# Loading the next batch ahead of the second attention pass, and starting a value group with its third token tile

## The chip, the cores and the metric

The kernel runs on one core of a Trainium2 chip. Its time is device microseconds (us) of one launch that works through all eight batches. A core has five instruction streams that run side by side and meet only at semaphores: TensorE (PE in the profile; PEld is its weight loads), VectorE (DVE), ScalarE (ACT), GpSimd (POOL) and SyncE (SP), which here issues nearly all transfers. The runs of the kernel before took 1346.44 us in the median of three (1345.10 to 1354.54).

## The reference, cut to what matters

Each of 8 batches is an image of 256 tokens and a text of 128 tokens, 256 features each, 384 tokens together.

```
# 1. image tokens: attention-free mixing
k, v, q = projections of x                       # x[b] is (64 features, 256 tokens, 4 heads)
num, den = exp(w_bias * mask) @ (exp(k) * v), exp(w_bias * mask) @ exp(k)
h_img = layernorm(sigmoid(q) * num / den @ out_w + out_b + x) * ln_g + ln_b
# 2. text tokens: rows of an embedding table
h_txt = W_E[tokens] * sqrt(256)
h = concat(h_img, h_txt)                         # 384 x 256
# 3. attention, 16 heads of 16, with relative keys and values in a window of +-4
s = q k^T + band(q, emb_rel_k);  p = softmax(s)
h = h + (p v + band(p) emb_rel_v) @ Wo + bo
# 4. eight experts with routing weights
h = h + sum_e w_e * (silu(x Wg_e) * (x Wu_e)) @ Wd_e
```

Batches don't depend on one another.

## The kernel before, in words

**Two batches in flight.** While a batch b goes through mixing and attention, the experts of the batch before, f = b - 1, are worked off in between, as units of matmul work with which TensorE fills the waits of the attention. The order of steps is written out by `schedule(attention, ffn)`: one list, which each engine walks, taking from it the steps for which it has a function. `rounds` (L399) puts it on an engine three times: once for batch 0 without experts, then as the body of a hardware loop `engine.Fori(1, NB)` over b = 1 to 7 with the experts of b - 1, and once more for the experts of batch 7 alone. So the loop's body runs seven times. `later(b)` tells the loop (b is a register) from batch 0 (b is a number): in the loop buffers have earlier users that must be waited for.

**One body, in order.** It begins with `residual` of batch f (output projection of its attention, L849, after the last accumulation of the experts before it, L1320), then `mix_in` of batch b: the tokens `x_in` and the text's indices `txt_idx` are transferred (L482, L483, issued by SP) and eight fp32 matmuls for exp(k), exp(k)v (L646) and four for q (L651, two records each) read x_in. Then `turn_x2` (L627 and, before it, DVE's normalisation L1075), `mix_sums`, `router`, `mix_out`, whose matmuls (L681, L684) are the last to read x_in and raise the seventh count of `mix_pe`. GpSimd gathers the text rows with the indices (L1364), scales them (L1373), and takes the roots of the normalisations (L1351, L1354). Then come the projections of q, k, v, a trip of q, k and of the relative scores through DRAM, with 20 expert units over it, the **first pass** (`maxima`, 24 items: scores for the row maxima), and the negated maxima (`negate`, in two halves, each sent to DRAM and back into two extra rows of q_st, L589 and L592).

**The second pass**, `attend`, again has 24 items. An item is two 128x384 score tiles of a head pair: TensorE multiplies (L794), VectorE adds the window of relative scores (L1187, two instructions), ScalarE takes the exponential into `p_t` (L996) and raises `exp_done`. Three pairs of PSUM banks are used in turn, so item n waits for the exponential of item n - 3. `tiles_of(n)` gives the tiles: three items hold the three token tiles (0, 1, 2) of two heads; the first holds tiles 0 and 1 of a head, the second tile 2 of both heads, the third tiles 0 and 1 of the other. No experts are worked on in this pass. Each six items (four heads) are followed by a **value group** g of three steps, `values(b, g, i)` for the token tiles i = 0, 1, 2: each is four matmuls of 17 columns of weights, for four heads, that sum over i in one bank (L809; eight records). Group g is placed behind the items 7 + 6g, 8 + 6g and 9 + 6g; its first step waits for all 6(g + 1) exponentials. Group 3 comes behind the last item, its three steps in a row. ScalarE copies each finished group (L1000). GpSimd copies the windows of p_t into `bands` (L1434), two instructions for each head pair.

**Behind the second pass** `turn_outputs` waits for the last copy. SP sends the windows to DRAM and back in another layout (L600, L609), and `turn_weights` (DVE L1207, then TensorE) takes them. Between these steps lie the last expert units of batch f. The body ends with `store` on SP (L616), which waits for the last accumulation. SP works in order, so in the next turn of the loop the transfer of x_in is issued behind that store:

```
def mix_in(b):                                   # SP, L477
    if later(b):
        sp.wait_ge(mix_pe.sem, mix_pe.at(b - 1, 7))
        sp.wait_ge(txt_loaded.sem, txt_loaded.at(b - 1, 1))
    sp.dma_start(x_in[0:F, :, :], a["x"][b]).then_inc(x_loaded.sem, 16)
    sp.dma_start(txt_idx[:], a["txt_t"][b]).then_inc(idx_loaded.sem, 16)
```

Of the kernel before, what the change touches and what calls it, by code (L numbers as in the profile page):

```python
# [33 lines left out]
NB = 8  # L34
F, L, H = 64, 256, 4
# [4 lines left out]
TT = T // P  # L40
IT = L // P
AH, AD = 16, 16
# [24 lines left out]
GRP = 4  # L67
PTS = 6
# [12 lines left out]
FILL_MAXIMA = [0, 0, 0, 1, 0, 0, 0, 1, 0, 0, 0, 1, 0, 0, 0, 1, 0, 0, 0, 1, 0, 0, 0, 0]  # L81
FILL_NEGATE = 2
# [18 lines left out]
def fusion_block(nc, a, out):  # L101
# [14 lines left out]
    with ctx:  # L116
# [203 lines left out]
        def schedule(attention, ffn):  # L320
# [50 lines left out]
            flush()  # L371
            for n in range(ITEMS):
                steps.append(("attend", n, dict(seen)))


                g, at = divmod(n - 7, 6)
                if g >= 0 and at < TT:
                    steps.append(("values", g, at, dict(seen)))
                if n >= 9 and (n - 9) % 6 == 0:
                    steps.append(("copy", (n - 9) // 6))  # L380
            last = AH // GRP - 1
            steps += [("values", last, i, dict(seen)) for i in range(TT)] + [("copy", last)]
# [16 lines left out]
        def rounds(engine, parts):  # L399
# [9 lines left out]
            with engine.Fori(1, NB) as b:  # L409
                for s in schedule(True, True):  # L410
                    do(s, b, b - 1)
            for s in schedule(False, True):
                do(s, None, NB - 1)
# [8 lines left out]
        def later(b):  # L422

            return not isinstance(b, int)
# [5 lines left out]
        def _(sp):  # L430
# [45 lines left out]

            def mix_in(b):  # L477

                if later(b):
                    sp.wait_ge(mix_pe.sem, mix_pe.at(b - 1, 7))  # L480
                    sp.wait_ge(txt_loaded.sem, txt_loaded.at(b - 1, 1))
                sp.dma_start(x_in[0:F, :, :], a["x"][b]).then_inc(x_loaded.sem, 16)  # L482
                sp.dma_start(txt_idx[:], a["txt_t"][b]).then_inc(idx_loaded.sem, 16)  # L483
                if not later(b):
                    load(1)
# [132 lines left out]
            rounds(sp, {"mix_in": mix_in, "prepare": prepare, "project_rel": project_rel,  # L618
# [6 lines left out]
        def _(pe):  # L625
# [172 lines left out]
            def values(b, g, i, seen):  # L798

                if i == 0:  # L800
                    pe.wait_ge(exp_done.sem, exp_done.at(b, 6 * (g + 1)))
# [5 lines left out]
                for l in range(GRP):  # L807
                    h = GRP * g + l
                    mm = pe.matmul(S[32 * l:32 * l + VC, 6 + g % 2, 0:T], v_one[:, i, h, :],  # L809
                                   p_t[:, h % PTS, i, :], start=(i == 0), stop=(i == TT - 1),  # L810
                                   skip_group_check=True)
                if i == TT - 1:
                    mm.then_inc(pv_done.sem, 1)
# [228 lines left out]
        def _(dve):  # L1042
# [267 lines left out]
            def accumulate(f, e, part):  # L1310
# [4 lines left out]
                if last and part == 0 and not isinstance(f, int):  # L1315
# [167 lines left out]
```

## Time and profile before

| | |
|---|---|
| time, median of 3 runs | 1346.44 us (1345.10 to 1354.54) |
| the profiled execution | 1361.19 us, its span 1359.4 us |
| TensorE busy, of the span | 1139.8 us, 84% |
| VectorE, ScalarE, GpSimd busy | 750.2, 370.3, 234.3 us |
| granted TensorE clock, mean | 0.896 of full speed |
| stores of the batches 0 to 6 issued at | 327.43, 484.87, 645.17, 802.26, 964.96, 1123.16, 1279.74 us |

The profile is of one execution, which was 14.75 us above the median of the timed runs. A timeline row gives start, duration, engine, line and operation, and in brackets how long the engine had been idle before it and what ended that. A granted clock of 1.00 is TensorE at 2.4 GHz, 0.50 at 1.2 GHz. The distance between two stores is one turn of the loop: 156.6 to 162.7 us.

### The profile page before, as it was taken

The page shows a single profiled execution, that of the slowest core. Times are in us where ns is not written, and L with a number is a line of the kernel's source. Part 1 is how long each engine was busy: PE and PEld are TensorE (multiplying, and loading weights), DVE is VectorE, ACT ScalarE, POOL GpSimd, SP SyncE. Part 2 cuts the span into 40 slices and gives each one's busy share as a digit, 9 for nine tenths or more (in the row PEclk, how much of TensorE's full clock was granted, in tenths as well). Part 3 has the DMA queues.
Part 4 walks back from the last instruction along what each step waited for, and adds up shares of the span by engine and source line. Part 5 has one row for each costly group of instructions (what it writes and reads, how often), then busy time and mean ns, then how long its engine had stood idle before and what let it go on. Part 6 is the DMA issues. An engine that isn't in the chain of part 4 may idle for free.

```text
span 1359.4 us, 16898 instructions
## 1 busy us (share of the span) xinstructions
PE 1139.8 (84%) x5668; PEld 801.1 (59%) x5668; DVE 750.2 (55%) x1579; ACT 370.3 (27%) x599; POOL 234.3 (17%) x258
## 2 busy tenths in 40 slices
PE   5447689878898798988899788997999889898798
PEld 4311379526784377735785277852787457762587
DVE  6336363673547546484546735485454745567443
ACT  1204312062211622134120621216121351205211
POOL 5404220031200402012200412004020122003100
PEclk9667779898999988899898987998889997999989
DMA  6592207402092102901065020921119010460200
GB/s 221 145 202 77 44 5 111 107 1 60 1 168 49 36 24 54 162 1 36 24 103 114 1 59 0 164 54 29 30 48 168 2 36 24 84 133 1 47 0 12
DMA packets 126842, 89.59 MB, mean 66 GB/s; under 512 B 67847, under 2 KB 116360, under 8 KB 126378
## 3 DMA queue, kind: packets, MB, share of 16 engines
q1 hardware_dynamic: 126408, 88.05, 31.9%
q0 software_dynamic: 384, 1.05, 0.3%
q14 instruction: 39, 0.32, 0.1%
q8 instruction: 11, 0.18, 0.1%
HBM read 60.36 MB, written 28.71 MB: 66 GB/s over the span
## 4 chain that ended last, share of the span: by engine, by line
PE 32%; issue 26%; DVE 15%; DMA 12%; SPq 6%; ACT 5%; POOL 3%; POOLq 0%; DVEq 0%; ACTq 0%
DMA scratch<-d_band_t 9%; PE S L878 7%; PE S L754 5%; PE S L746 4%; DVE S L1187 4%; PE S L899 4%; SPq L538 4%; PE S L809 4%; ACT scratch L996 3%; PE S L710 3%; DVE maxima L1166 3%; PE S L794 2%; DMA txt_row<-in_L_txt_W_E,txt_idx 1%; PE S L627 1%; DMA w_d<-in_L_ffn_Wu 1%
## 5 line engine op out<-in xcount | busy, mean ns | idle before, releaser
L1166 DVE TENSOR_REDUCE maxima<-S 128x2 f32<-128x768 f32 x192 | 177.1, 954 | 86.7 <-PE S L754 83.9
L1434 POOL TENSOR_TENSOR bands<-scratch,one 64x432 f32<-64x432 f32 x128 | 119.7, 935 | 598.3 <-ACT scratch L996 593.2
L899 PE MATMUL S<-w_d,hT 128*128 128x256 f32 x768 | 189.4, 395 | 1.6 <-DVE hT L1308 0.7
L746 PE MATMUL S<-k_st,q_st 128*128 128x384 bf16 x384 | 140.7, 366 | 49.3 <-DMA scratch<-d_band_t 35.6
L1033 ACT ACTIVATE silu<-S 128x384 f32<-128x384 f32 x128 | 63.0, 492 | 436.2 <-PE S L878 382.1
L1187 DVE TENSOR_TENSOR S<-S,bands 64x144 f32<-64x144 f32 x384 | 154.5, 402 | 44.7 <-PE S L794 35.0
L996 ACT ACTIVATE scratch<-S 128x768 f32<-128x768 f32 x192 | 155.7, 812 | 56.6 <-DVE S L1187 49.2
L899 PEld LDWEIGHTS S<-w_d,hT 128*128 128x128 f32 x768 | 150.5, 199 | 25.0 <-issue 3.7
L754 PE MATMUL S<-scratch,ident_b 128*128 128x132 bf16 (+1 forms) x384 | 155.0, 404 | 0.0
L1308 DVE TENSOR_TENSOR hT<-silu,S 128x384 f32<-128x384 f32 x128 | 70.7, 552 | 130.5 <-PE S L878 120.7
L794 PE MATMUL S<-q_st,k_st 128*128 128x384 bf16 x384 | 94.0, 344 | 35.7 <-ACT scratch L996 34.5
L809 PE MATMUL S<-scratch,v_one 128*17 128x384 f32 x768 | 91.9, 574 | 27.4 <-ACT scratch L996 27.1
L746 PEld LDWEIGHTS S<-k_st,q_st 128*128 128x128 bf16 x384 | 39.5, 103 | 120.2 <-DVE maxima L1166 59.0
L1320 DVE SCALAR_TENSOR_TENSOR res<-S,wgt,res 128x256 f32<-128x256 f32 x168 | 75.4, 480 | 48.3 <-PE S L899 48.0
L794 PEld LDWEIGHTS S<-q_st,k_st 128*128 128x128 bf16 x384 | 25.6, 98 | 122.5 <-ACT scratch L996 92.5
L878 PE MATMUL S<-x_hi,wu_hi 128*128 128x384 f32 x256 | 77.1, 384 | 15.0 <-DVE hT L1308 15.0
L878 PE MATMUL S<-x_hi,wg_hi 128*128 128x384 f32 x256 | 81.7, 402 | 0.0
L627 PE MATMUL S<-ident,scratch 128*128 128x128 f32 (+1 forms) x196 | 36.7, 338 | 42.9 <-DVE scratch L1075 28.6
L878 PE MATMUL S<-x_lo,wg_hi 128*128 128x384 f32 x256 | 68.9, 352 | 0.0
L878 PE MATMUL S<-x_hi,wg_lo 128*128 128x384 f32 x256 | 68.5, 350 | 0.0
L878 PE MATMUL S<-x_lo,wu_hi 128*128 128x384 f32 x256 | 68.1, 348 | 0.0
L878 PE MATMUL S<-x_hi,wu_lo 128*128 128x384 f32 x256 | 67.9, 347 | 0.0
(157 smaller groups left out, 1488.4 us busy)
## 6 DMA issues: line engine op xcount, KB each, us to landing
bands<-d_band_s SPq DMA_DIRECT2D x16, 864.0 KB, 8.7
scratch<-d_band_t SPq DMA_DIRECT2D x8, 1632.0 KB, 16.9
d_parts<-scratch SPq DMA_DIRECT2D x48, 192.0 KB, 2.0
q_st<-d_parts SPq DMA_DIRECT2D x48, 192.0 KB
k_st<-d_parts SPq DMA_DIRECT2D x48, 192.0 KB
d_band_w<-bands SPq DMA_DIRECT2D x32, 240.0 KB, 3.8
out<-scratch SPq DMA_DIRECT2D x8, 384.0 KB, 2.5
x_in<-in_x SPq DMA_DIRECT2D x8, 256.0 KB, 3.6
```

The source lines that it names most:

```text
L746: pe.matmul(S[:, bank, PAD:PAD + T], q_st[:, h, i * P:(i + 1) * P], k_st[:, h, :], start=True, stop=False, skip_group_check=True)
L754: mm = pe.matmul(S[rows, bank, at + w0:at + w1], ident_b[rows, rows], band_t[rows, i, w0:w1, h], start=False, stop=True, skip_group_check= ...
L794: mm = pe.matmul(S[:, 2 * (n % 3) + l, PAD:PAD + T], k_st[:, h, i * P:(i + 1) * P], q_st[:, h, :], start=True, stop=True)
L809: mm = pe.matmul(S[32 * l:32 * l + VC, 6 + g % 2, 0:T], v_one[:, i, h, :], p_t[:, h % PTS, i, :], start=(i == 0), stop=(i == TT - 1), skip ...
L878: mm = pe.matmul(dst[:, 0:T], ws[:, e, k, m * P:(m + 1) * P], xs[:, k, :], start=(j == 0), stop=(j == 3 * KT - 1))
L899: mm = pe.matmul(D[:, i // 2, (i % 2) * E:(i % 2 + 1) * E], hT[:, (FT * e + m) % 3, i * P:(i + 1) * P], w_d[:, e, m, :], start=(m == 0), s ...
L996: nc.scalar.activation(dst, S[:, c0:c0 + 2, PAD:PAD + T], ACT.Exp).then_inc(exp_done.sem, 1)
L1166: dve.tensor_reduce(dst, S[:, c0:c0 + 2, PAD:PAD + T], AX, ALU.max).then_inc(max_done.sem, 1)
L1187: dve.tensor_tensor(win, win, band, ALU.add).then_inc(sc_add.sem, 1)
L1308: dve.tensor_tensor(hT[:, n % 3], silu[:], U[:, 0:T], ALU.mult).then_inc(h_done.sem, 1)
L1320: dve.scalar_tensor_tensor((out_st if last else res)[:, i], D[:, i // 2, (i % 2) * E:(i % 2 + 1) * E], wgt[:, i, e:e + 1], res[:, i], ALU. ...
L1434: nc.gpsimd.tensor_tensor(bands[rows, :, :, 2 * pair:2 * pair + 2].rearrange("p i w h -> p h i w"), win, one[rows].unsqueeze(2).unsqueeze( ...
```

## The change

The step list gets a new step `fetch` between the negated maxima and the second pass: SP then transfers the tokens and indices of batch b + 1, after waiting for `mix_out` and the text gather of batch b. `mix_in` keeps the transfer for batch 0 only. Batch 7 has nothing to fetch, so the loop runs to b = 6, and the turn b = 7 is written out behind it with `more=False`. Within a value group the order of token tiles is 2, 0, 1. The first step (tile 2) waits for one exponential fewer, the second for all of the group; the accumulation starts with tile 2 and ends with tile 1. In group 3 tile 2 comes right behind the last item. `later` now also holds for a number above zero, and a wait in VectorE's last accumulation holds for f = 6 as it did in the loop.

```diff
+VALUE_TILES = (2, 0, 1)
...
-        def schedule(attention, ffn):
+        def schedule(attention, ffn, more=True):
...
             fill(FILL_NEGATE)
             flush()
+            if more:
+                steps.append(("fetch",))
             for n in range(ITEMS):
                 steps.append(("attend", n, dict(seen)))
+                if n == ITEMS - 1:
+                    steps.append(("values", AH // GRP - 1, VALUE_TILES[0], dict(seen)))
                 g, at = divmod(n - 7, 6)
                 if g >= 0 and at < TT:
-                    steps.append(("values", g, at, dict(seen)))
+                    steps.append(("values", g, VALUE_TILES[at], dict(seen)))
                 if n >= 9 and (n - 9) % 6 == 0:
                     steps.append(("copy", (n - 9) // 6))
             last = AH // GRP - 1
-            steps += [("values", last, i, dict(seen)) for i in range(TT)] + [("copy", last)]
+            steps += [("values", last, i, dict(seen)) for i in VALUE_TILES[1:]] + [("copy", last)]
...
-            with engine.Fori(1, NB) as b:
+            with engine.Fori(1, NB - 1) as b:
                 for s in schedule(True, True):
                     do(s, b, b - 1)
+            for s in schedule(True, True, False):
+                do(s, NB - 1, NB - 2)
...
-            return not isinstance(b, int)
+            return not isinstance(b, int) or b > 0
...
-            def mix_in(b):
-
-                if later(b):
-                    sp.wait_ge(mix_pe.sem, mix_pe.at(b - 1, 7))
-                    sp.wait_ge(txt_loaded.sem, txt_loaded.at(b - 1, 1))
+            def load_x(b):
                 sp.dma_start(x_in[0:F, :, :], a["x"][b]).then_inc(x_loaded.sem, 16)
                 sp.dma_start(txt_idx[:], a["txt_t"][b]).then_inc(idx_loaded.sem, 16)
+
+            def fetch(b):
+
+                sp.wait_ge(mix_pe.sem, mix_pe.at(b, 7))
+                sp.wait_ge(txt_loaded.sem, txt_loaded.at(b, 1))
+                load_x(b + 1)
+
+            def mix_in(b):
+
                 if not later(b):
+                    load_x(b)
                     load(1)
                     load(2)
...
             def values(b, g, i, seen):
-                if i == 0:
-                    pe.wait_ge(exp_done.sem, exp_done.at(b, 6 * (g + 1)))
+                if i != VALUE_TILES[-1]:
+
+                    pe.wait_ge(exp_done.sem, exp_done.at(b, 6 * (g + 1) - (i == VALUE_TILES[0])))
+                if i == VALUE_TILES[0]:
                     if g >= 2:
                         pe.wait_ge(o_copied.sem, o_copied.at(b, g - 1))
...
-                                   p_t[:, h % PTS, i, :], start=(i == 0), stop=(i == TT - 1),
+                                   p_t[:, h % PTS, i, :], start=(i == VALUE_TILES[0]), stop=(i == VALUE_TILES[-1]),
                                    skip_group_check=True)
-                if i == TT - 1:
+                if i == VALUE_TILES[-1]:
                     mm.then_inc(pv_done.sem, 1)
...
-                if last and part == 0 and not isinstance(f, int):
+                if last and part == 0 and not (isinstance(f, int) and f == NB - 1):
```

## Rows read from the trace of the kernel before

**Rows 1.** The page: busy time of the engines; ScalarE's exponentials.
```profile
PE 1139.8 (84%) x5668; PEld 801.1 (59%) x5668; DVE 750.2 (55%) x1579; ACT 370.3 (27%) x599; POOL 234.3 (17%) x258
...
L996 ACT ACTIVATE scratch<-S 128x768 f32<-128x768 f32 x192 | 155.7, 812 | 56.6 <-DVE S L1187 49.2
```

**Rows 2.** TensorE's waits, 169 to 1286, seven turns: total, times, longest.
```profile
PE S L794 <- ACT scratch L996: 32.0, 62, 1.2
PE S L809 <- ACT scratch L996: 24.1, 26, 2.4
...
PE S L646 <- DMA x_in<-in_x: 11.8, 6, 2.0
```

**Rows 3.** Timeline at a turn's start: start, us, engine, line [idle before].
```profile
327.31 2.86 PE L849 MATMUL S<-w_o,scratch 128*128 128x256 f32 x12 [1.03 <-DVE scratch L1320]
...
328.50 0.55 SPq L482 DMA_DIRECT2D x_in<-in_x  x1
...
332.07 4.10 PE L646 MATMUL S<-wkv,x_in 65*128 65x128 f32 x16 [1.91 <-DMA x_in<-in_x]
...
332.51 0.86 POOL L1354 TENSOR_TENSOR rstd<-rstd,neg_half 128x3 f32<-128x3 f32 x1
...
336.10 2.06 PE L651 MATMUL S<-x_in,wq_t 65*64 65x256 f32 x8
...
336.96 1.15 DVE L1075 TENSOR_SCALAR scratch<-res,mv,rstd 128x256 f32<-128x256 f32 x3
...
338.17 1.54 PE L627 MATMUL S<-ident,scratch 128*128 128x128 f32 x6
```

**Rows 4.** Timeline, the last transfer of `negate` before the second pass, batch 2.
```profile
436.25 0.23 SPq L592 DMA_DIRECT2D q_st<-d_neg  x1
```

**Rows 5.** The tile x_in: from issue to landing.
```profile
DMA to landing us min/median/max: 3.4/3.6/3.7
```

**Rows 6.** Timeline of a second pass: first items, value groups 0 to 2.
```profile
437.34 1.24 PE L794 MATMUL S<-q_st,k_st 128*128 128x384 bf16 x6
...
444.17 0.84 PE L809 MATMUL S<-scratch,v_one 128*17 128x384 f32 x8 [0.46 <-ACT scratch L996]
...
444.94 0.50 PE L794 MATMUL S<-q_st,k_st 128*128 128x384 bf16 x2
...
450.48 0.84 PE L809 MATMUL S<-scratch,v_one 128*17 128x384 f32 x8 [0.32 <-ACT scratch L996]
...
456.87 0.84 PE L809 MATMUL S<-scratch,v_one 128*17 128x384 f32 x8 [0.41 <-ACT scratch L996]
```

**Rows 7.** Timeline, end of second passes: last exponentials, value group 3.
```profile
461.48 1.65 ACT L996 ACTIVATE scratch<-S 128x768 f32<-128x768 f32 x2
...
463.26 3.82 PE L809 MATMUL S<-scratch,v_one 128*17 128x384 f32 x24 [2.39 <-ACT scratch L996]
...
1259.82 2.13 PE L809 MATMUL S<-scratch,v_one 128*17 128x384 f32 x24 [2.38 <-ACT scratch L996]
```

**Rows 8.** Timeline, the windows' way back: batch 2 in the loop, batch 0.
```profile
471.05 1.80 SPq L609 DMA_DIRECT2D scratch<-d_band_w  x3
...
477.12 0.67 DVE L1207 TENSOR_TENSOR scratch<-scratch 128x216 f32<-128x216 f32 x2
...
153.86 1.76 SPq L609 DMA_DIRECT2D scratch<-d_band_w  x3
...
158.01 0.68 DVE L1207 TENSOR_TENSOR scratch<-scratch 128x216 f32<-128x216 f32 x2 [4.82 <-DMA scratch<-d_band_w]
```

**Rows 9.** Stretches, two turns and group 3: us, busy by engine, clock, DMA, GB/s.
```profile
649.82:806.98 157.16, 136.33 (x709) 96.00 (x709) 91.52 (x196) 45.20 (x74) 24.92 (x30) 0.95 0.32 60
806.98:969.62 162.64, 143.43 (x709) 100.42 (x709) 91.43 (x195) 45.41 (x74) 24.87 (x30) 0.88 0.31 58
...
463.20:467.70 4.50, 3.83 (x25) 0.95 (x25) 0.00 (x0) 0.54 (x2) 1.86 (x2) 0.62 0.36 75
```

**Rows 10.** DMA queue that brings instructions, 325 to 490: packets, MB, share.
```profile
q14 instruction: 7, 0.06, 0.1%
```

More of the change, by code:

```diff
@@ L616, in store @@
                 sp.dma_start(out[f].rearrange("(i p) e -> p i e", p=P), out_st).then_inc(stored.sem, 16)
-            rounds(sp, {"mix_in": mix_in, "prepare": prepare, "project_rel": project_rel,
+            rounds(sp, {"mix_in": mix_in, "fetch": fetch, "prepare": prepare, "project_rel": project_rel,
                         "weights": weights, "negate": negate, "turn_weights": windows_back,
```

## The prediction

> **What bounds the kernel now.** I read the page first. TensorE is busy for 84% of the span and no other engine reaches 60% [rows 1]. So the kernel is near TensorE's own work, and what an edit can win is a hole in TensorE that nothing refills. The list of waits tells which holes exist. In the seven turns of the loop the largest are waits for ScalarE's exponentials, ahead of the items of the second pass (32.0 us) and ahead of the value groups (24.1 us), then for x_in (11.8 us) [rows 2]. The change touches the second and the third. The timelines then say where each hole lies and what stands behind it.
>
> **Part 1, the tokens of the next batch.** At a turn's start TensorE ends the output projection about 330.2 (327.31 + 2.86) and then stands until 332.07, because SP issued x_in only at 328.50, behind the store [rows 3]; the landing takes 3.6 us [rows 5], and 328.50 + 3.6 is 332.1. The waits are six in number, 1.9 to 2.0 us each, 11.8 us in sum [rows 2]. The seventh turn start, b = 1, has no such wait, because batch 0 has no experts and no store, so nothing is counted there. After the change x_in has landed long before, and the matmuls L646 begin at 330.2.
>
> Is the shift kept? Behind L646 come L651 (336.10) and the transposes L627 (338.17), which follow L651 without a hole (336.10 + 2.06 = 338.16) [rows 3]. The transposes need DVE's normalisation L1075, which stood at 336.96 behind the products of exp(k); those follow L646 and move with it. It also needs GpSimd's roots, done at 333.37 (332.51 + 0.86), where the moved L1075 wants them at 335.0, so there are 1.6 us to spare [rows 3]. GpSimd's gather of the text stands behind those roots in an unchanged order and needs no x_in; the first reader of its rows is the statistics of the whole batch, behind mix_out. I take the full 11.8 us. The ends are 0, if a second late operand stands right behind, and 11.8 plus nothing: more than the wait can't come out of the wait.
>
> What the moved step costs where it goes: per batch two waits and two transfers on SP behind the last transfer of `negate`, at 436.5 [rows 4]. Both waits are for steps that lie before the projections and the first pass, so nothing queued behind them is held; SP's next own step is the windows' way out, behind the last exponential at 463.1 [rows 7]. 256 KB in flight for 3.6 us share the queues with the small transfer of the negated maxima, issued just ahead and needed in its second half only from item 12, over 10 us on. Cost 0; were that cover gone it would be at most the 3.6 us of one landing.
>
> **Part 2, the first wait of value groups 0 to 2.** The first step of a group stood 0.46, 0.32 and 0.41 us for an exponential [rows 6], in sum 1.19 us a pass. With tile 2 first the exponential it needs is one that the item ahead of it has already waited for, so the wait is gone; the step takes 0.77 us (444.17 to the next item at 444.94) [rows 6], and in that time the missing exponential ends, which the next item and the second step need. So the next item starts 0.4 us earlier and, since TensorE is then the engine the others wait for (0.77 us of values ahead of each of three items), the whole chain behind it moves. I followed the recurrence item by item (TensorE 0.43 us for an item, DVE 0.85, ScalarE 0.83, a step 0.77, three bank pairs, the copy and the gate of p_t slots included): it gives 25.8 us from the first item to the last exponential where the trace has 25.8 (437.34 [rows 6] to 463.13 [rows 7]), and 24.6 with the new order. So 1.2 us a pass is kept. ScalarE's own work doesn't stop it: 24 exponentials of 0.81 us are 19.5 us [rows 1].
>
> **Part 3, value group 3.** Before, TensorE stood 2.39 us until the last exponential, then ran three steps in 3.82 us [rows 7]. The exponentials of the last two items are back to back (461.48, 1.65 us for two), so the last but one ends about 0.8 us before the last [rows 7], and a step of 0.77 us fits into that. Two steps remain behind the last exponential instead of three: the gain is a third of the group's time. Over the eight passes that time is 3.72, 3.68, 3.82 (four times), 3.17 and 2.13 us. It is 3.82 where the granted clock is at its low level, 1.2 GHz, for most of it (mean 0.62 from 463.2 on [rows 9]) and 2.13 at 2.4 GHz. In the seven loop passes the sum is 24.3 us, a third of it 8.1.
>
> Is it kept behind the pass? The last copy, `turn_outputs` and expert units follow on TensorE. What runs in parallel is the windows' way: GpSimd's last windows, SP's two trips. It starts with the last exponential, so it moves by 1.2 us, while TensorE moves by 1.2 plus 0.7 to 1.3. In batch 0 the second trip is issued at 153.86 and DVE gets it at 158.01, 4.15 us on [rows 8]; in the loop 471.05 + 4.15 is 475.2, and DVE takes it at 477.12 [rows 8], so 1.9 us are to spare and at least 0.6 stay. Kept in the loop. In batch 0, without expert units, that way is itself the path (DVE waits 4.82 us for it [rows 8]), so only the 1.2 us of part 2 count there.
>
> **Part 4, the last turn written out.** The same instructions with numbers in place of registers, and one jump back fewer. At the jump TensorE waited 1.03 us, and for DVE's last accumulation, not for instructions [rows 3]; I count 0, with 0 to 1.03 as bounds on the good side. On the bad side there is new code to bring in: seven packets of instructions in a turn, of 8 KB each [rows 10]. They come in loop turns as well, under running work. The Trainium skill ("Runtime: NRT & Kernel Launch", Instruction fetch mechanics) says that a taken branch breaks the sequential prefetch and forces a fetch before execution goes on; by it the missing jump would add a little to the gain. No row here shows such a stall, so the sum goes without it.
>
> **The sum.** 11.8 (x_in) + 7 x 1.19 = 8.3 (groups 0 to 2) + 8.1 (group 3) + 1.2 (batch 0) = 29.4 us. The profiled execution of 1361.19 us would come to 1331.8. It stood 14.75 us, 1.1%, above the median; against the median of 1346.44 the same 29.4 us give **1317 us**. All parts act on waits that exist in every execution, only group 3 depends on the clock.
>
> **The clock is the unknown size.** Two turns with the same 709 matmuls took 157.16 and 162.64 us, at mean granted clocks of 0.95 and 0.88 [rows 9]. The three timed runs lie 9 us apart. A change that moves work by 2 to 4 us a turn changes where the low stretches fall. If every loop turn fell like the shortest, the six turns from 327.43 to 1279.74, 158.7 on average, would each give 1.6 us more, 11 us over seven; if like the longest, they would lose 3.9 each, 27 us. The Trainium skill ("TensorE: Matmul & The Clock Gate", Part 1) says that for modelling the ramp's penalty is under 1% of a typical span. By that both ends would stay within 13 us. The trace differs: 5.5 us between two turns is 3.4% of a turn. I keep the wider bounds for the rivals and half of them for the likeliest case.
>
> **Rivals.**
> 1. *The second pass gives its share back.* Items wait for ScalarE 32.0 us already [rows 2]; if removed group waits reappear ahead of items, parts 2 and 3 bring nothing and only x_in remains: 1346.4 - 11.8 = 1335. For it: the pass is a ring of three engines, and each group's wait is for the engine that also gates the items. Against it: the items behind a group's steps start without a wait [rows 6], so there TensorE leads. Chance 0.10.
> 2. *More than the waits.* Fewer holes, so the clock stays up: 1317 - 11 = 1306. For it: at a second pass's end, behind a hole of 2.39 us, the mean was 0.62 [rows 7, 9]. Against: the low stretches at turn starts also came after holes that stay (1.03 us [rows 3]). Chance 0.10.
> 3. *The clock takes it back.* All turns fall like the longest: 1317 + 27 = 1344. Against: turns differ among each other and will again. Chance 0.06.
> 4. *Slower: fetching the written-out turn.* Its code runs once, straight through, on five engines. If each of its 8 KB packets held TensorE for a landing like x_in's, 3.6 us [rows 5], the seven of a turn would cost 25 us [rows 10], and twice as many packets (straight code is not kept) 50 us: 1317 + 50 = 1367. It decides from nine held packets on (29.4 + 1% of 1346 is 43 us, twelve packets, for slower by over 1%). Against: batch 0 is straight code too, and its second pass has the same group waits and period as the loop's. Chance 0.04.
>
> **How the numbers follow.** The forecast, both parts kept, has 0.70; its own range is 1309 to 1331, half the clock bounds around 1317. The range to give takes in rivals 1 and 2: 1303 to 1336; about 0.12 lies outside, mostly rivals 3 and 4. A measurement of this kernel tells about 1% from no change, so faster means under 1333: the forecast and rival 2 and a small part of rival 1, 0.82. Within 1%: the rest of rival 1, rival 3 and a tail, 0.14. Slower: 0.04.
>
> **What the profile after would show.** TensorE's wait for x_in is gone, and L646 follows L849 at once; SP's L482 of the next batch stands right behind L592. The first step of value groups 0 to 2 starts without a wait, a second pass takes 24.6 us from first item to last exponential, and group 3 appears as one step ahead of the last exponential and two behind it. Wrong would be: a wait of some 2 us for another releaser ahead of L646 or ahead of L627 at 1075's place; waits ahead of L794 grown by what L809's fell; DVE's L1207 waiting for the windows in the loop; a hole of TensorE without a releaser in the last turn.

## The result and the profile after

The changed kernel takes 1300.18 us (median of 4 runs, 1298.56 to 1307.80), the kernel before 1350.49 us beside it: a ratio of 0.966, with a 95% interval of 0.960 to 0.971. Timed again in five rounds it took 1299.09 us, ratio 0.964 (0.959 to 0.969). The ratio leaves out runs over 1.5% above the kernel's fastest, here the 1361.05 us of the kernel before, and gives 46 to 48 us; the medians alone give 50. The forecast said 29. So its 1317 us had the direction and missed the size, and its range, 1303 to 1336, ended 3 us above the measured median.

The page after: VectorE, ScalarE and GpSimd are busy within 2 us as long as before. TensorE is busy 31 us less (1139.8 to 1109.1) with the same 5668 matmuls, so they ran faster. Of the 62 us between the two profiled executions the other 31 are TensorE's holes (span less busy time, 219.6 to 188.2). Two lines of the page, the first answering to [rows 1]:

```profile
PE 1109.1 (85%) x5668; PEld 787.9 (61%) x5668; DVE 748.5 (58%) x1579; ACT 369.6 (28%) x599; POOL 233.8 (18%) x258
...
L824 PE MATMUL S<-scratch,v_one 128*17 128x384 f32 x768 | 81.3, 507 | 12.3 <-ACT scratch L1011 12.3
```

TensorE's waits after, in seven turns (160 to 1230), answering to [rows 2], and behind them two of the kernel before (169 to 1286) that [rows 2] leaves out. Total, times, longest:

```profile
PE S L807 <- ACT scratch L1011: 32.3, 63, 1.2
PE S L640 <- DVE scratch L1090: 18.5, 8, 4.3
PE S L824 <- ACT scratch L1011: 10.8, 7, 1.6
...
PE S L759 <- DMA scratch<-d_band_t: 4.6, 5, 1.3
...
PE S L627 <- DVE scratch L1075: 14.3, 7, 2.1
...
PE S L746 <- DMA scratch<-d_band_t: 11.0, 7, 3.4
```

The wait for x_in is gone, that ahead of the value groups fell from 24.1 to 10.8 us and occurs seven times instead of 26, and the items' own waits (now L807) did not grow: 32.0 before, 32.3 after. That settles rival 1: nothing was given back inside the second pass. The wait ahead of the transposes (L627, now L640) did not change either: 14.3 us in seven turns, and 4.3 us once behind them, at 1225.63, for the last batch's experts, where no mixing lies between.

The wait for the relative scores (`d_band_t`, the transfer ahead of the first pass) fell from 11.0 to 4.6 us, and neither part of the change touches it. It is 2.4 us in the profile of experiment 1, which has every wait of the kernel before, so it differs by 8.6 us between executions of the same work. The difference of 6.4 us is not to be counted for the change.

The turn's start after, answering to [rows 3]; the matmuls on x_in are now L659 and L664, the transposes L640:

```profile
467.60 2.86 PE L864 MATMUL S<-w_o,scratch 128*128 128x256 f32 x12 [1.03 <-DVE scratch L1335]
470.29 3.85 PE L659 MATMUL S<-wkv,x_in 65*128 65x128 f32 x16
474.07 2.06 PE L664 MATMUL S<-x_in,wq_t 65*64 65x256 f32 x8
476.06 1.54 PE L640 MATMUL S<-ident,scratch 128*128 128x128 f32 x6
```

L659 follows L864 without a hole, and from the output projection to the transposes it is 8.46 us, against 10.86 before. The transfer stands where it was put, behind the negated maxima [rows 4]:

```profile
423.02 0.23 SPq L605 DMA_DIRECT2D q_st<-d_neg  x1
423.59 0.55 SPq L485 DMA_DIRECT2D x_in<-in_x  x1
```

The same second pass as in [rows 6] and [rows 7], after. It begins at 424.02, and the first steps of groups 0, 1 and 2 carry no wait:

```profile
424.02 1.24 PE L807 MATMUL S<-q_st,k_st 128*128 128x384 bf16 x6
...
430.32 0.84 PE L824 MATMUL S<-scratch,v_one 128*17 128x384 f32 x8
431.10 0.50 PE L807 MATMUL S<-q_st,k_st 128*128 128x384 bf16 x2
...
436.23 0.84 PE L824 MATMUL S<-scratch,v_one 128*17 128x384 f32 x8
...
442.15 0.84 PE L824 MATMUL S<-scratch,v_one 128*17 128x384 f32 x8
...
447.71 2.22 PE L824 MATMUL S<-scratch,v_one 128*17 128x384 f32 x24 [1.56 <-ACT scratch L1011]
```

Groups 0 to 2 now follow each other in 5.9 us (430.32, 436.23, 442.15) where they took 6.3 and 6.4. Group 3 starts behind a hole of 1.56 us and takes 2.22 us instead of 3.82. Where each turn of the loop spends less can be read from the first rows of each stage. The table has the seven turns in sum, from the timelines of four profiled executions: before (1361.19 us), experiment 1 (the same waits as before, 1337.44 us), after (1299.13 us) and experiment 12 (the changed kernel again, 1298.74 us).

| stretch of a turn | before | exp. 1 | after | exp. 12 |
|---|---|---|---|---|
| output projection to mix_sums | 85.5 | 85.4 | 69.8 | 69.8 |
| mix_sums to the projections of q, k | 215.8 | 214.4 | 210.8 | 213.0 |
| projections to the first pass | 246.6 | 238.4 | 239.8 | 240.2 |
| first pass | 198.2 | 188.4 | 189.7 | 189.8 |
| to the second pass | 37.3 | 33.7 | 36.8 | 35.5 |
| second pass with group 3 | 208.8 | 210.3 | 185.7 | 182.6 |
| behind it | 123.9 | 124.2 | 124.0 | 123.8 |

The first row is the fetch, the sixth the order of tiles. The rows between them were touched by neither part. They lose 21 us from before to after, but the profiled execution of before was one of its slower ones; against experiment 1, the fastest of its runs, they lose nothing that two executions of one kernel do not differ by. So most of the gain lies in the two rows that the change touches: 15.7 us in the first and 23 to 28 in the sixth, 39 to 43 together, where the forecast had 11.8 and 16.4, or 28. The medians of all runs differ by 50 us, so some 7 to 11 us of a typical execution lie in other stretches; these four profiles don't show where.

Turns of the loop after, with the clock, against [rows 9]; and group 3:

```profile
467.60:617.60 150.00, 134.82 (x708) 96.90 (x708) 91.20 (x195) 45.14 (x74) 24.80 (x30) 0.97 0.33 63
768.80:919.10 150.30, 135.61 (x709) 96.12 (x709) 91.18 (x195) 45.05 (x74) 24.82 (x30) 0.97 0.33 63
447.70:450.50 2.80, 2.22 (x24) 0.50 (x24) 0.00 (x0) 1.18 (x2) 1.86 (x2) 1.00 0.00 0
```

The mean granted clock of the whole execution is 0.93, against 0.896. In group 3 it is 1.00, against 0.62 in [rows 9].

### The profile page after: what moved, and what is told of

Read it like the earlier page. It is cut to its first block, busy times and chain, and to the rows that moved or that the text cites. A ratio compares the mean times of both kernels' runs of the same rounds, so it can differ in the third digit from the quotient of the medians.

```text
span 1297.3 us, 16627 instructions
## 1 busy us (share of the span) xinstructions
PE 1109.1 (85%) x5668; PEld 787.9 (61%) x5668; DVE 748.5 (58%) x1579; ACT 369.6 (28%) x599; POOL 233.8 (18%) x258
## 4 chain that ended last, share of the span: by engine, by line
PE 40%; issue 22%; DVE 16%; DMA 10%; SPq 5%; ACT 4%; POOL 3%; POOLq 0%; DVEq 0%; ACTq 0%
PE S L893 10%; DMA scratch<-d_band_t 6%; PE S L914 6%; PE S L767 5%; PE S L759 4%; DVE S L1202 4%; PE S L824 4%; PE S L723 3%; DVE maxima L1181 3%; PE S L807 3%; SPq L551 3%; ACT scratch L1011 3%; PE S L640 2%; DMA txt_row<-in_L_txt_W_E,txt_idx 1%; DMA w_d<-in_L_ffn_Wu 1%
## 5 line engine op out<-in xcount | busy, mean ns | idle before, releaser
L914 PE MATMUL S<-w_d,hT 128*128 128x256 f32 x768 | 184.4, 388 | 1.4 <-DVE hT L1323 0.7
L759 PE MATMUL S<-k_st,q_st 128*128 128x384 bf16 x384 | 134.4, 350 | 45.0 <-DMA scratch<-d_band_t 29.8
L1011 ACT ACTIVATE scratch<-S 128x768 f32<-128x768 f32 x192 | 155.5, 811 | 44.9 <-DVE S L1202 37.3
L914 PEld LDWEIGHTS S<-w_d,hT 128*128 128x128 f32 x768 | 147.8, 195 | 23.8 <-issue 2.3
L807 PE MATMUL S<-q_st,k_st 128*128 128x384 bf16 x384 | 93.1, 341 | 36.1 <-ACT scratch L1011 34.8
L807 PEld LDWEIGHTS S<-q_st,k_st 128*128 128x128 bf16 x384 | 25.6, 98 | 122.1 <-ACT scratch L1011 96.3
L824 PE MATMUL S<-scratch,v_one 128*17 128x384 f32 x768 | 81.3, 507 | 12.3 <-ACT scratch L1011 12.3
L893 PE MATMUL S<-x_hi,wu_hi 128*128 128x384 f32 x256 | 76.8, 382 | 12.9 <-DVE hT L1323 12.8
L893 PE MATMUL S<-x_hi,wg_hi 128*128 128x384 f32 x256 | 80.8, 397 | 0.0
L640 PE MATMUL S<-ident,scratch 128*128 128x128 f32 (+1 forms) x196 | 34.2, 321 | 45.2 <-DVE scratch L1090 28.6
L893 PE MATMUL S<-x_lo,wu_hi 128*128 128x384 f32 x256 | 68.6, 350 | 0.0
L893 PE MATMUL S<-x_hi,wu_lo 128*128 128x384 f32 x256 | 68.4, 350 | 0.0
L893 PE MATMUL S<-x_lo,wg_hi 128*128 128x384 f32 x256 | 67.7, 346 | 0.0
L893 PE MATMUL S<-x_hi,wg_lo 128*128 128x384 f32 x256 | 66.4, 341 | 0.0
```

Of the source, the lines that this page charges most:

```text
L759: pe.matmul(S[:, bank, PAD:PAD + T], q_st[:, h, i * P:(i + 1) * P], k_st[:, h, :], start=True, stop=False, skip_group_check=True)
L807: mm = pe.matmul(S[:, 2 * (n % 3) + l, PAD:PAD + T], k_st[:, h, i * P:(i + 1) * P], q_st[:, h, :], start=True, stop=True)
L893: mm = pe.matmul(dst[:, 0:T], ws[:, e, k, m * P:(m + 1) * P], xs[:, k, :], start=(j == 0), stop=(j == 3 * KT - 1))
L914: mm = pe.matmul(D[:, i // 2, (i % 2) * E:(i % 2 + 1) * E], hT[:, (FT * e + m) % 3, i * P:(i + 1) * P], w_d[:, e, m, :], start=(m == 0), s ...
L1011: nc.scalar.activation(dst, S[:, c0:c0 + 2, PAD:PAD + T], ACT.Exp).then_inc(exp_done.sem, 1)
```

## The experiments

The theory under test, "waits and clock": each closed hole gives its own length, and the rest comes from TensorE spending less time at 1.2 GHz. Rivals: "waits only", and for the missing 17 us the code written out.

**1. The last turn written out and nothing else.** The kernel before, with:

```diff
-            with engine.Fori(1, NB) as b:
+            with engine.Fori(1, NB - 1) as b:
                 for s in schedule(True, True):
                     do(s, b, b - 1)
+            for s in schedule(True, True):
+                do(s, NB - 1, NB - 2)
...
-            return not isinstance(b, int)
+            return not isinstance(b, int) or b > 0
...
-                if last and part == 0 and not isinstance(f, int):
+                if last and part == 0 and not (isinstance(f, int) and f == NB - 1):
```

> The kernel before with its seventh loop turn written out and nothing else. The whole change gained about 46 us (ratio 0.966) where the removed waits explain 29. Theory 'waits and clock' (each hole closed gives its own length, and the rest comes from TensorE staying at its high clock): this kernel has every hole of before, so 1350 us, ratio 0.995 to 1.005. Rival 'written-out code' (the missing 17 us come from the straight turn): ratio about 0.987. Rival 'straight code must be fetched': ratio over 1.005.

Measured: 1349.24 us, ratio 1.0004 (0.997 to 1.004). Neither a gain nor a cost of fetching the written-out turn beyond the interval, 5 us each way; rival 4 (25 to 50 us) and the rival for the missing part (17 us) both fall. Its runs also showed how far one and the same program spreads, 1337 to 1363 us.

**2. The fetch alone.** Tokens ahead, value groups in the old order; against the changed kernel:

```diff
-VALUE_TILES = (2, 0, 1)
+VALUE_TILES = (0, 1, 2)
...
-                if n == ITEMS - 1:
-                    steps.append(("values", AH // GRP - 1, VALUE_TILES[0], dict(seen)))
...
-            steps += [("values", last, i, dict(seen)) for i in VALUE_TILES[1:]] + [("copy", last)]
+            steps += [("values", last, i, dict(seen)) for i in VALUE_TILES] + [("copy", last)]
...
-                if i != VALUE_TILES[-1]:
-
-                    pe.wait_ge(exp_done.sem, exp_done.at(b, 6 * (g + 1) - (i == VALUE_TILES[0])))
+                if i == VALUE_TILES[0]:
+                    pe.wait_ge(exp_done.sem, exp_done.at(b, 6 * (g + 1)))
```

> Tokens fetched ahead and the last turn written out; value groups in the old order 0, 1, 2. Theory 'waits only': the six waits of L646, 11.8 us, so ratio 0.991. Theory 'waits and clock': more than the waits, 15 to 22 us, ratio 0.984 to 0.989, with TensorE's low-clock time clearly under the 284 us of the profile before.

Measured: 1324.29 us, ratio 0.979 (0.974 to 0.984): 28 to 29 us for waits of 11.8 us, more than the 15 to 22 that "waits and clock" had expected. Value group 3, behind its old hole of 2.4 us, is as slow as before in five of the seven turns (3.58 to 3.82 us) and takes 2.13 us in two. The first of the slow ones:

```profile
297.13 3.58 PE L821 MATMUL S<-scratch,v_one 128*17 128x384 f32 x24 [2.37 <-ACT scratch L1008]
```

**3. The order alone.** The kernel before with `values` and the step list of the change, x_in as before, all turns in the loop.

> Only the order of the value tiles (2, 0, 1); tokens loaded as before, all seven turns in the loop. Theory 'waits only': 8.3 + 8.1 + 1.2 = 17.6 us, ratio 0.987. Theory 'waits and clock': 23 to 32 us, ratio 0.976 to 0.983, with value group 3 in 2.2 us instead of 3.8 in most turns.

Measured: 1318.69 us, ratio 0.9755 (0.971 to 0.980), 33 us for 17.6 of waits and a step. Here second passes, counted from the first item to the end of group 3, take 25.9 to 26.0 us in five of seven turns; with the whole change it is four of seven in the first profile and six of seven in experiment 12. By the ratios the two parts won 29 and 33 us alone and 46 to 48 together. Waits that lie in different stages would be expected to add up; that these don't fits a clock that both parts raise, but does not show it.

**4. Group 3 late again, in the changed kernel.**

```diff
-                    pe.wait_ge(exp_done.sem, exp_done.at(b, 6 * (g + 1) - (i == VALUE_TILES[0])))
+                    pe.wait_ge(exp_done.sem, exp_done.at(b, 6 * (g + 1) - (i == VALUE_TILES[0] and g < 3)))
```

> The changed kernel, but the first step of value group 3 again waits for the last exponential, so three steps follow it in a row behind a hole of 2.4 us; groups 0 to 2 and the fetch stay. Theory 'waits only': it loses the 8 us of one step a turn against the changed kernel, ratio to before 0.972. Theory 'waits and clock': the hole of 2.4 us lowers the clock again, group 3 takes 3.8 us, and it loses 14 us or more, ratio 0.976 or above.

Measured: 1303.81 us, ratio 0.966 (0.960 to 0.972). Both theories missed: against the changed kernel it costs 4 to 5 us by the medians and 0 to 2 by the ratios, which is not clear of the noise and less than either said. Its timeline at group 3, in four of the seven turns:

```profile
295.43 2.13 PE L824 MATMUL S<-scratch,v_one 128*17 128x384 f32 x24 [2.38 <-ACT scratch L1011]
444.78 2.13 PE L824 MATMUL S<-scratch,v_one 128*17 128x384 f32 x24 [2.39 <-ACT scratch L1011]
595.68 2.13 PE L824 MATMUL S<-scratch,v_one 128*17 128x384 f32 x24 [2.38 <-ACT scratch L1011]
...
896.92 3.44 PE L824 MATMUL S<-scratch,v_one 128*17 128x384 f32 x24 [2.39 <-ACT scratch L1011]
```

The hole is as long as before, and yet the group runs at the high clock (1.00 from 444.70 to 447.50), in six of the seven turns. So the hole of 2.4 us by itself does not bring the low clock; something ahead of it has to be as it was. Experiment 2 narrows it down: it too has the fetch and this hole, but groups 0 to 2 wait as before, and there group 3 is slow in five of seven turns. What differs is groups 0 to 2, which in experiment 2 start behind waits of 0.3 to 0.5 us and here without (and the order of the tiles in them).

**5. Holes filled, waits kept.** The kernel before; TensorE multiplies into a bank that the next matmul overwrites, ahead of L646 and ahead of group 3. No wait is shortened.

```diff
+            def busy(bank, n):
+                for _ in range(n):
+                    pe.matmul(S[:, bank, 0:E], w_o[:, 0, 0:P], w_o[:, 0, :], start=True, stop=True,
+                              skip_group_check=True)
...
+                if later(b):
+                    busy(0, 3)
                 pe.wait_ge(x_loaded.sem, x_loaded.at(b, 1))
...
+                if i == 0 and g == 3:
+                    busy(7, 4)
+                    pe.wait_ge(exp_done.sem, exp_done.at(b, 6 * (g + 1)))
```

> The kernel before, with both waits left in place but filled: three idle-result fp32 matmuls (128x128 by 128x256, some 1.4 us) in TensorE's hole ahead of L646 in the loop turns, and four (some 1.9 us) in the hole of 2.4 us ahead of value group 3. Their results are overwritten. No wait of the change is shortened. Theory 'waits and clock': the clock stays up more, and at least a third of the 46 us comes back without any edit of the waits: ratio 0.975 to 0.99. Theory 'waits only': 0 or a little slower, ratio 0.998 to 1.005.

Measured: 1335.87 us, ratio 0.988 (0.984 to 0.992). This shows the clock's part without any change of the waits: work that nobody needs, put into two of them, makes the kernel 16 us faster.

**6. Groups 0 to 2 late again, in the changed kernel.** `i == VALUE_TILES[0] and g == 3` in the place of experiment 4's condition.

> The changed kernel, but the first step of value groups 0 to 2 waits for all of its group's exponentials as before; fetch and the early step of group 3 stay. Part 2 of the sum was 8.3 us: 'waits only' expects 0.6 points more than the changed kernel, ratio 0.972. 'Waits and clock' expects the second pass to be 1.2 us longer a turn and the low clock to come back at group 3 in part of the turns: ratio 0.972 to 0.978.

Measured: 1312.29 us, ratio 0.970 (0.967 to 0.974), 12 to 13 us slower than the changed kernel by the medians, 6 to 8 by the ratios, where the sum had 8.3. TensorE's waits ahead of L824 are 18.5 us again, 27 times. Second passes take 27.3 us in six of seven turns, 1.4 longer than with the change. The low clock did not come back at group 3, as "waits and clock" had expected: group 3 takes 2.2 to 2.3 us in every turn, and the mean clock of the runs, 0.931, is above the changed kernel's 0.926. TensorE also waits 13.8 us ahead of expert units (L893), against 10.3, but that wait is 10.9 to 14.2 us in profiles of kernels with every wait of before.

**7. Holes filled in the changed kernel.** `busy` ahead of the output projection (2), of the transposes of the normalised tokens (3) and of group 3's early step (2).

> The changed kernel with idle-result fp32 matmuls in three holes that are left: two ahead of the output projection, three ahead of the transposes of the normalised tokens, two ahead of the early step of group 3. 'Waits and clock': low-clock time falls below the 184 us of the changed kernel's profile and the time by up to 10 us, unless the added matmuls delay the path: ratio 0.96 to 0.968. 'Waits only': 0 to 5 us slower, ratio 0.966 to 0.970.

Measured: 1304.51 us, ratio 0.964 (0.960 to 0.968). The ratio lies inside the range of "waits and clock", but its interval holds the changed kernel's own, so this tells nothing apart. The mean clock did not rise either (0.928 in the profiled execution, against 0.930 and 0.926 in the two of the changed kernel), so filling these holes gave nothing that can be measured.

**8. One expert unit earlier, in the changed kernel.** `("router_pick", 2)` in the place of 1.

> The changed kernel with one more expert unit behind router_pick, in TensorE's hole of 2.1 us ahead of the transposes, and so one fewer at the turn's end. Every theory: 1.0 us a turn is won if the hole takes it, about 7 us, ratio 0.960; if VectorE's accumulation, which then comes ahead of its normalisation, delays that, nothing or a loss: 0.966 to 0.970.

Measured: 1330.97 us, ratio 0.985 (0.981 to 0.988): 31 us slower than the changed kernel. TensorE's waits in seven turns show why; two of these rows the changed kernel does not have, VectorE's accumulation ahead of the transposes and the negated maxima ahead of an expert's down part:

```profile
PE S L893 <- DVE hT L1323: 16.3, 13, 1.7
PE S L640 <- DVE res L1335: 11.5, 6, 1.9
PE S L640 <- DVE scratch L1090: 9.6, 7, 1.4
...
PE S L914 <- DVE neg_max L1186: 8.5, 7, 1.2
```

A unit moved at one place shifts every later one, and other kinds of unit then stand at the tight places: between the passes a turn needs 8.0 us instead of 5.3, and the seven first passes 204.8 us instead of 189.7. Of the 32 us between the profiled executions 27 are TensorE's holes (215.1 against 188.2), and 5 are matmuls that ran slower.

**9 and 10. Each hole filled alone, in the kernel before.** Experiment 5 without `busy(0, 3)`, and without `busy(7, 4)`.

> The kernel before with only the hole ahead of value group 3 filled (four fp32 matmuls whose result is overwritten), all waits as before. With both holes filled the ratio was 0.988. If the clock lost at group 3 is what the filling wins, each turn's second pass is 1.7 us shorter (28.0 against 29.7 us) and the ratio 0.990 to 0.993; if the hole at the turn's start is the one that counts, 0.996 to 1.001.

> The kernel before with only the hole ahead of L646 filled (three fp32 matmuls whose result is overwritten), x_in still waited for. If the idle TensorE at the turn's start is what pulls the clock down in the mixing stage, ratio 0.990 to 0.995 and low-clock time from a turn's start to the projections of 10 us a turn instead of the 14 to 20 in every other turn of before; if not, 0.998 to 1.003.

Measured: group 3 alone 1334.60 us, ratio 0.9895 (0.982 to 0.997); the turn's start alone 1355.50 us, ratio 1.002 (0.999 to 1.006). The gain of filling lies at group 3; at the turn's start it is 2 us at most, by the interval. Its timeline there, with the four matmuls (L640, eight records) in the hole:

```profile
451.44 0.82 PE L799 MATMUL S<-q_st,k_st 128*128 128x384 bf16 x4
452.11 1.89 PE L640 MATMUL S<-w_o 128*128 128x256 f32 x8
454.60 2.13 PE L818 MATMUL S<-scratch,v_one 128*17 128x384 f32 x24 [0.60 <-ACT scratch L1005]
```

The group is released as late as before and takes 2.13 us instead of 3.82. Its stretch shows the granted clock at 1.00:

```profile
454.50:457.30 2.80, 2.13 (x24) 0.60 (x24) 0.00 (x0) 0.54 (x2) 1.88 (x2) 1.00 0.00 0
```

It won 14 us by the ratio (4 to 24 by its interval), where seven groups of 1.7 us less make 12. At the turn's start the filling was there too, leaving 0.6 to 1.0 us of the wait:

```profile
479.33 1.46 PE L640 MATMUL S<-w_o 128*128 128x256 f32 x6
481.38 2.83 PE L653 MATMUL S<-wkv,x_in 65*128 65x128 f32 x11 [0.59 <-DMA x_in<-in_x]
```

Here the clock did rise, from a mean of 0.74 to 0.79 in the old turn starts to 0.87 to 0.91 in six of the seven, between the output projection and mix_sums, and it bought nothing: these turns need 12.1 to 12.5 us to mix_sums as before. x_in still lands when it did, L646's matmuls ran at the high clock for the most part already (4.10 us against 4.00), and the transposes behind them wait up to 0.15 us for VectorE. In the turn b = 1, which has no such wait, the three matmuls are plain extra work and cost 1.3 us.

**11. Mixing ahead of the output projection.** The early tokens allow it: in the step list `mix_in` comes first, with the waits that the shared banks and GpSimd's windows then need.

```diff
-FILL_MIX = [("residual", 0), ("mix_in", 0), ("turn_x2", 0), ...
+FILL_MIX = [("mix_in", 0), ("residual", 0), ("turn_x2", 0), ...
...
+                if later(b):
+                    pe.wait_ge(att_dve.sem, att_dve.at(b - 1, 2 * TT + 2 * KT))
                 pe.wait_ge(x_loaded.sem, x_loaded.at(b, 1))
...
                     pool.wait_ge(hid_ready.sem, hid_ready.at(b - 1, 5))
+                    pool.wait_ge(win_done.sem, win_done.at(b - 1, WINS * AH // 2))
```

> The changed kernel with mix_in ahead of residual in the step list, which the early tokens now allow (the needed waits for the relative values' sum and for GpSimd's windows are added). The six matmuls groups on x_in, 5.8 us, then run while VectorE ends the last accumulation, so the hole of 1.03 us ahead of L864 closes, and the mixing chain starts 3.9 us earlier. Expected: 1 to 3 us a turn, ratio to before 0.950 to 0.961. If the normalisation of the residual and so the first expert units come too late instead: 0.966 or above.

Measured: 1343.23 us, ratio 0.991 (0.987 to 0.996), 43 us slower than the changed kernel. The timeline of its turn start:

```profile
479.55 4.00 PE L661 MATMUL S<-wkv,x_in 65*128 65x128 f32 x16
483.48 2.05 PE L666 MATMUL S<-x_in,wq_t 65*64 65x256 f32 x8
485.46 5.21 PE L866 MATMUL S<-w_o,scratch 128*128 128x256 f32 x12
495.29 1.54 PE L640 MATMUL S<-ident,scratch 128*128 128x128 f32 x6 [4.62 <-DVE scratch L1092]
```

The hole of 1.03 us did close in the loop. But in the old place the 6 us of mixing covered the way from the output projection through statistics, roots and normalisation to the transposes. Now TensorE stands 4.62 us there (4.6 in each of the seven turns, 32 us in all), and the projection itself runs at the low clock (mean granted clock 0.54 from 485.4 to 490.7), 5.21 us instead of 2.86 here.

**12. The changed kernel once more.**

> The changed kernel as it is, timed in as many rounds as the experiments, since its first four runs leave open whether the late group 3 (ratio 0.966, median 1303.8 us) costs anything at all. If the early step of group 3 is worth the 8.1 us of the sum, this kernel stands at 1295 to 1298 us; if it is worth only a step at the high clock, 0.7 us a turn, at 1299 to 1302 us. Theory 'waits and clock': its runs lie some 25 to 29 us under the line of time against granted clock that the runs of the kernel before give, at a mean clock near 0.927.

Measured: 1299.09 us (1295.06 to 1307.30), the second case: the early step of group 3 is worth 4 to 5 us by the medians, though the intervals of the two ratios overlap.

## Why the prediction came out right in direction and short in size

**The clock's share.** Each run comes with its mean granted clock. Over all 62 runs of the kernel before and 12 of experiment 1, time falls in a straight line with the clock, 2164.9 - 901.7 x clock, and the runs scatter 2.4 us around it, at clocks of 0.890 to 0.917. The distance of another kernel's runs from that line is what it wins at equal clock; the rest is clock. The line is drawn on by 0.01 for the changed kernel's mean. The profiles bear it out for this pair: it gives 31 us for clocks of 0.896 and 0.930, and TensorE's busy time differs by 31.

| kernel | mean of runs, us | clock | against the line, us | by the clock, us |
|---|---|---|---|---|
| before (62 runs) | 1352.3 | 0.901 | 0 | 0 |
| changed (10) | 1300.8 | 0.926 | -28.9 | -22.4 |
| fetch alone (6) | 1324.5 | 0.918 | -12.3 | -15.5 |
| order alone (6) | 1319.3 | 0.922 | -14.7 | -18.2 |
| group 3 late, exp. 4 (6) | 1305.7 | 0.924 | -25.8 | -20.7 |
| groups 0 to 2 late, exp. 6 (6) | 1311.0 | 0.931 | -14.6 | -26.6 |
| group 3 filled (6) | 1336.0 | 0.924 | +3.8 | -20.0 |
| start filled (12) | 1355.5 | 0.907 | +8.3 | -5.0 |

At equal clock the change wins 28.9 us; the sum was 29.4. A line through the 64 runs that took less than 1359.9 us has a slope of -819 and splits the gain into 30.5 and 19.4. What failed is the step "the clock is the unknown size": I kept it at zero in the likeliest case, with 8 us downwards (half of its own 11 would have been 5.5), and it gave 19 to 22 us. Rival 2, with a chance of 0.10 and 1306 us, was the nearest case.

The split has an error that the filled kernels show. No wait of theirs was moved, and yet they lie 4 and 8 us above the line. At the turn's start 1.3 us of it is the extra work of b = 1, and the rest fits a higher clock in a stretch where it wins no time (experiment 10), which raises the mean all the same; for the 4 us no reason was found. So single terms are good to some us only.

That 28.9 and 29.4 agree so well is luck in part. By the same line groups 0 to 2 are worth 14.3 us (experiment 6 against the changed kernel), where the sum had 9.5 (8.3, and 1.2 in batch 0; the passes themselves show 1.4 us, ten in seven turns), and the early step of group 3 is worth 3.1 (experiment 4), where it had 8.1. The fetch, 12.3 us alone, is where 11.8 stood. By this measure two terms were wrong by 5 us, one each way.

**Part 1, the tokens.** Right in its mechanism. The wait is gone, nobody else was late, and the matmuls on x_in start 2.1 us earlier in the turn; the transposes start 2.4 us earlier, where 1.9 was forecast, since L646 also runs in 3.85 instead of 4.10 us. The whole stretch to mix_sums wins 15.7 us in seven turns instead of 11.8; 11.8 of them are holes. One reading was wrong without harm: x_in's is not the third largest wait of the loop. In [rows 2]'s list 14.3 us ahead of the transposes (L627) and 12.5 ahead of expert units (L878) come before it.

**Part 2, the first wait of groups 0 to 2.** Right in kind. A pass is 27.3 us with late groups (experiment 6) and 25.9 without: 1.4 us where I had 1.2. From the first item to the last exponential it is 24.4 us in the pass shown (424.02 to 448.39), and 24.6 was forecast.

**Part 3, group 3.** The step that failed in its size. I took a third of 3.82 us, as though the low clock belonged to the group. The passes of the experiments take it apart: 29.7 us before; 28.0 with the hole filled, so 1.7 us is the clock; 26.7 with groups 0 to 2 early and group 3 late (experiment 4); 25.9 with all of it, so the early step itself is 0.7 us, a step at the high clock. A turn of this kind wins 3.8 us here, where the sum had 2.3 (8.3 and 8.1 over seven turns): 1.4 + 0.7 + 1.7. In the profile after three of seven passes take 27.2 to 27.5 us, with the low clock elsewhere in them, so that the seven win 23 us in sum and not 27. Over seven turns the clock's part at group 3 is up to 12 us, a little over half of the 19 to 22.

**Was it kept behind the pass?** TensorE moved by 3.8 us and the windows' way by 1.2, so the spare 1.9 us of [rows 8] was used up. In the profile after VectorE waits for the windows in every loop turn but the last, at 460.71 for 0.66 us; TensorE, with expert units in between, waits for it twice: in batch 0, 6.4 us instead of 4.3, and once for 0.2 us in the loop:

```profile
156.12 0.68 DVE L1222 TENSOR_TENSOR scratch<-scratch 128x216 f32<-128x216 f32 x2 [6.92 <-DMA scratch<-d_band_w]
309.23 0.68 DVE L1222 TENSOR_TENSOR scratch<-scratch 128x216 f32<-128x216 f32 x2 [1.37 <-DMA scratch<-d_band_w]
460.71 0.68 DVE L1222 TENSOR_TENSOR scratch<-scratch 128x216 f32<-128x216 f32 x2 [0.66 <-DMA scratch<-d_band_w]
```

That is the sign I had named as wrong, and it is there, without a cost to TensorE in most turns. "At least 0.6 stay" took the pass to win 1.9 to 2.5 us a turn, and it won 3.8. It is what ends next if the second pass gets shorter still.

**Part 4, the turn written out.** Right: nothing (experiment 1). What the Trainium skill ("Runtime: NRT & Kernel Launch", Instruction fetch mechanics) says of a taken branch shows in no measurement here.

**The bound on the clock.** I had weighed the statement of the Trainium skill ("TensorE: Matmul & The Clock Gate", Part 1) that the ramp's penalty is under 1% of a typical span. That sentence stands where the page describes the first rise of the clock, and I had used it as a bound on what later falls can do. In that use the measurement decides against it: the clock's part of the change is 19 to 22 us, 1.5 to 1.7% of 1300, and one kernel's runs spread by 2% along the line of time against clock. No run here measures the first rise by itself.

**Open.** Why the fetch raises the clock (15 us by the line) is not settled. It isn't the filled hole: filling that hole with matmuls brought nothing. In the profiles the low stretches behind a turn's start and in the first pass come and go from turn to turn, so that the effect may come from where the turn's later stages fall; nothing here tells that from other causes. Why the short waits ahead of groups 0 to 2 decide at which clock group 3 runs behind the same hole of 2.4 us (slow in five of seven turns in experiment 2, in one of seven in experiment 4) is open as well; that they do rests on these two kernels and one profile of each.

## What to carry to other kernels

Take a matmul kernel's holes at their own length and then ask separately what the clock does behind each; where a run's mean granted clock is known, draw time against clock over the repeats of one kernel and compare another with it at equal clock. Set the result beside busy time and holes of the profiles, and beside a second profile of the kernel before: a stretch that the change does not touch can differ by 8 us between two executions. Before counting a group of matmuls as slow, look at the granted clock in its stretch: a hole ahead of it may have made it slow, and throwaway matmuls in the hole tell so. A higher clock is worth something only where TensorE sets the pace. A step whose operands have come early should not be moved up for that alone: in its old place it may be the cover of another chain, as the mixing was.

## What the runs showed of the hardware

Eight fp32 matmul records on operands nobody needed, in a wait of 2.4 us, made the 24 records behind them take 2.13 instead of 3.82 us and the kernel 1.1% faster (ratio 0.982 to 0.997). Three such matmuls (six records) in a wait of 1.9 us at a turn's start left the kernel's time as it was. The kernel before ran in 1339 to 1364 us, along one line with its mean granted clock: 0.01 of the mean clock is 8 to 9 us here.
